# An eight-layer kernel whose expert routing moves into the layers beside it, in two halves, with three wide products split by columns

## The chip, the cores and the metric

One core of a Trainium2 chip runs the whole program. The metric is the device time of one execution in microseconds, taken as the median of several runs. The engines are TensorE (PE; its weight loads are shown as PEld), VectorE (DVE), ScalarE (ACT), GpSimd (POOL) and SyncE (SP, which starts DMAs). Each runs its own instructions in order and waits for the others on semaphores.

## The reference, cut to what matters

Sixteen sequences of 256 tokens with 128 channels go through eight residual layers: a wide attention (16 heads of 64), the experts, a "slope" attention, the same experts again, a "rope" attention, a "group" attention, a recurrence, and the group attention once more. The change touches the first four.

```python
x = x + _L0_attn_a_ref(_layernorm(x, axis=-1), ...)   # wide attention
x = x + _L0_ffn_ref(_layernorm(x, axis=-1), ...)      # experts
x = x + _L0_attn_b_ref(_layernorm(x, axis=-1), ...)   # slope attention
x = x + _L0_ffn_ref(_layernorm(x, axis=-1), ...)      # experts
x = x + _L1_attn_a_ref(_layernorm(x, axis=-1), ...)   # rope attention
...
def _L0_ffn_ref(x, gate_w, w1, w2):
    cap = int(EXPERT_CAPACITY * T / E)                # 64 of 256 tokens for each of 8 experts
    scores = jnp.einsum('BTC,CE->BTE', x, gate_w)
    probs = jax.nn.softmax(scores, axis=-1)
    probs_et = jnp.transpose(probs, (0, 2, 1))
    top_p, top_idx = jax.lax.top_k(probs_et, cap)
    xin = jnp.take_along_axis(x[:, None, :, :], top_idx[..., None], axis=2)
    h = jax.nn.gelu(jnp.einsum('BElC,ECH->BElH', xin, w1), approximate=False)
    y = jnp.einsum('BElH,EHC->BElC', h, w2)
    y = y * top_p[..., None]
    ...
```

Routing is everything down to `top_k`: each expert takes the 64 tokens of a sequence that like it most. A sequence ("batch" below) is routed without the others, but only after the layer in front has finished it.

## The kernel before

The activations `K.X` stay in on-chip memory for the whole program, as 32 tiles of 128 tokens by 128 channels, two tiles to a batch. Layers follow one another as blocks. A block begins when every engine has left the one before.

**Wide attention** (`wide_attention`, order from `wide_slots` and `wide_walk`). The heads are worked in 8 pairs for each of 16 batches; a pair is a slot. In a slot PE runs `score` (L2078, L2082), the row maxima of a later pair (`max`, L2062), `value` (L2093), the softmax sums (`sum`, L2099), and last the products of the coming batch that share two PSUM banks: `qk` (L2049, in every slot), `v` (L2055, four slots of eight), the transposes `norm` (L2043, slot 4), and the output product `project` (L2107, slots 3 and 5). In slot 7 the products stand ahead of `value`. All of it but `max`, `turnmax` and the shift `pick` is float32, and a float32 product is two PE instructions. `score` and `max` contract over 64 rows of the array, two side by side. `value` and `sum` fill 64 columns, two side by side. `qk`, `v`, `norm` and `project` use all 128 by 128.

**Routing** (`route`, a block of its own ahead of each experts' block). VectorE finishes the layer norm's statistics, normalizes all 32 tiles (L1463). PE transposes them (L1416), multiplies by the gate padded to 32 columns (L1423) and turns the logits back (L1431). VectorE does the softmax; PE turns the probabilities so that each of 128 partitions is one batch and expert. Then VectorE takes the 64 greatest in eight rounds of MAX8 and MATCH_REPLACE8 (L1492, L1493), turns the marks into slot numbers (L1494 to L1497), and PE turns those back (L1450). The probabilities and slots are `K.prob` and `K.slot`. Meanwhile ACT and POOL prepare the first two units of the experts (L1554, L1561 to L1564).

**Experts** (`experts`, order from `expert_schedule`). A unit is two batches. Step n has nine slots: `up` and `down` of unit n for each of 8 experts (L1636, L1644), and for unit n+1 the one-hot choice on VectorE (L1704) weighed on POOL (L1752), the gather (L1620) and four transposes (`turn`, L1627), and for unit n-1 the scatter (L1654). Step -1 only prepares unit 0. ACT does the GELU between `up` and `down`. At its start POOL first makes a counter and the constants of the coming attention (`pool_setup`).

**Slope attention** (`narrow_attention`, order from `NARROW_ORDER`). Eight slots for each batch, in which PE does `score` (L725, L732), `max` (L704, L711) and every second slot `value` (L745, 32 columns, four side by side); VectorE reduces the maxima (L911) and ACT takes the exponentials (L839). PE may not write new maxima before VectorE has reduced the old ones.

## Time and profile before

| what | value |
|---|---|
| median of 3 runs | 2300.91 us (2298.48 to 2302.19) |
| the profiled execution | 2305.23 us, span 2303.5 us |
| PE busy | 2030.9 us, 88% of the span |
| VectorE, ACT, POOL busy | 1557.1, 1174.0, 825.8 us |
| wide attention | from the start to about 655 us |
| routing and experts, first | about 656 to 880 us |
| slope attention | about 880 to 1124 us |
| routing and experts, second | from 1125 us |

The profiled execution is 4.3 us above the median of the runs, and its span lacks 1.7 us of its own time. Sums below are made on the span; what they take off it is taken off the median too. A matmul's row shows when it began and when its last result is there; since matmuls are pipelined, the distance from one row's start to the next row's start is what it took of PE.

### The profile page before, as it was taken

The page shows a single profiled execution, that of the slowest core. Times are in us where ns is not written, and L with a number is a line of the kernel's source. Part 1 is how long each engine was busy: PE and PEld are TensorE (multiplying, and loading weights), DVE is VectorE, ACT ScalarE, POOL GpSimd, SP SyncE. Part 2 cuts the span into 40 slices and gives each one's busy share as a digit, 9 for nine tenths or more (in the row PEclk, how much of TensorE's full clock was granted, in tenths as well). Part 3 has the DMA queues.
Part 4 walks back from the last instruction along what each step waited for, and adds up shares of the span by engine and source line. Part 5 has one row for each costly group of instructions (what it writes and reads, how often), then busy time and mean ns, then how long its engine had stood idle before and what let it go on. Part 6 is the DMA issues. An engine that isn't in the chain of part 4 may idle for free. (4 is left out here: it accounts for less than half of the span.)

```text
span 2303.5 us, 52488 instructions
## 1 busy us (share of the span) xinstructions
PE 2030.9 (88%) x20687; PEld 1356.6 (59%) x20687; DVE 1557.1 (68%) x2782; ACT 1174.0 (51%) x1972; POOL 825.8 (36%) x1276
## 2 busy tenths in 40 slices
PE   5999999999959997999589979997599985479996
PEld 3666666666638995665378966664345542335553
DVE  4777878787774444677554447775689965769983
ACT  3444444444323323666533326665478865447874
POOL 4444444444424341332144414440233322423330
PEclk9999999999979997999899989998699997769998
DMA  5000000000000011444000214440334420124441
GB/s 170 1 1 1 1 1 1 1 1 1 2 3 4 5 56 48 124 115 116 2 4 1 56 29 118 121 121 18 86 100 115 109 59 0 43 80 111 117 115 41
DMA packets 157126, 121.01 MB, mean 53 GB/s; under 512 B 13856, under 2 KB 129456, under 8 KB 156884
## 3 DMA queue, kind: packets, MB, share of 16 engines
q1 hardware_dynamic: 156884, 117.65, 18.9%
q8 instruction: 168, 2.75, 0.5%
q14 instruction: 74, 0.61, 0.1%
HBM read 63.48 MB, written 54.12 MB: 51 GB/s over the span
## 5 line engine op out<-in xcount | busy, mean ns | idle before, releaser
L911 DVE TENSOR_REDUCE l_group_mx<-maxima 128x4 f32<-128x1024 f32 x248 | 304.0, 1226 | 60.1 <-PE maxima L704 58.6
L839 ACT ACTIVATE l_group_pr<-scores 128x1024 f32<-128x1024 f32 x256 | 261.5, 1021 | 72.3 <-PE scores L725 69.9
L2195 POOL TENSOR_TENSOR l_wide_tiles_sum<-l_wide_pr 128x256 f32<-128x256 f32 x256 | 180.7, 727 | 212.4 <-ACT l_wide_pr L2138 212.4
L2166 DVE RECIPROCAL l_wide_rc<-bank 128x256 f32<-128x256 f32 x128 | 223.9, 1749 | 8.4 <-PE bank L2099 7.9
L2138 ACT ACTIVATE l_wide_pr<-scores 128x512 f32<-128x512 f32 x256 | 139.1, 595 | 163.1 <-PE scores L2082 163.1
L2150 DVE TENSOR_REDUCE l_wide_mx<-maxima 128x2 f32<-128x512 f32 x248 | 159.4, 685 | 52.7 <-PE maxima L2062 52.3
L2128 ACT ACTIVATE l_wide_qk<-bank 128x512 f32<-128x512 f32 x128 | 76.4, 597 | 174.9 <-PE bank L2049 174.8
L911 DVE TENSOR_REDUCE l_slope_mx<-maxima 128x6 f32<-128x768 f32 x124 | 118.9, 959 | 66.3 <-PE maxima L711 64.7
L911 DVE TENSOR_REDUCE l_rope_mx<-maxima 128x6 f32<-128x768 f32 x124 | 118.8, 958 | 44.0 <-PE maxima L711 42.8
L745 PE MATMUL bank<-l_group_pr,va 128*32 128x256 f32 x2048 | 143.9, 400 | 0.0
L839 ACT ACTIVATE l_slope_pr<-scores 128x768 f32<-128x768 f32 x128 | 103.5, 809 | 78.2 <-PE scores L732 78.0
L2093 PE MATMUL bank<-l_wide_pr,l_wide_va 128*64 128x256 f32 x1024 | 138.8, 392 | 0.0
L839 ACT ACTIVATE l_rope_pr<-scores 128x768 f32<-128x768 f32 x128 | 103.7, 810 | 64.7 <-PE scores L732 64.5
L2082 PE MATMUL scores<-l_wide_qk 64*128 64x256 f32 x1024 | 131.4, 376 | 0.0
L2190 POOL CAST l_wide_qk<-l_wide_qk 128x512 bf16<-128x512 f32 x128 | 78.1, 610 | 145.9 <-ACT l_wide_qk L2128 145.9
L704 PE MATMUL maxima<-l_group_st 50*128 50x256 bf16 x992 | 101.8, 285 | 30.8 <-DMA l_group_st<-mask_dram 15.0
L725 PE MATMUL scores<-l_group_st 53*128 53x256 bf16 x1024 | 103.0, 280 | 16.3 <-ACT l_group_pr L839 11.7
L1006 POOL CAST l_group_cols<-l_group_mx 128x32 bf16<-128x32 f32 x32 | 6.7, 209 | 307.7 <-DVE l_group_mx L911 307.7
L2082 PEld LDWEIGHTS scores<-l_wide_qk 64*128 64x128 f32 x1024 | 98.6, 189 | 9.8
L2049 PE MATMUL bank<-l_wide_xnt,w_q 128*128 128x256 f32 x256 | 90.3, 435 | 2.5 <-ACT l_wide_qk L2128 1.4
L1684 ACT ACTIVATE l_rope_e_ht<-maxima 128x512 f32<-128x512 f32 x64 | 38.2, 597 | 106.4 <-PE maxima L1636 106.0
L1684 ACT ACTIVATE l_slope_e_ht<-maxima 128x512 f32<-128x512 f32 x64 | 38.2, 597 | 104.0 <-PE maxima L1636 103.7
(478 smaller groups left out, 4779.6 us busy)
## 6 DMA issues: line engine op xcount, KB each, us to landing
l_group_st<-stack_dram SPq DMA_DIRECT2D x128, 192.0 KB, 3.9
l_slope_st<-stack_dram SPq DMA_DIRECT2D x64, 192.0 KB, 3.7
l_rope_st<-stack_dram SPq DMA_DIRECT2D x64, 192.0 KB, 3.8
stack_dram<-l_group_parts SPq DMA_DIRECT2D x64, 192.0 KB, 2.3
stack_dram<-l_group_parts SPq DMA_DIRECT2D x64, 128.0 KB, 1.9
stack_dram<-l_slope_parts SPq DMA_DIRECT2D x32, 192.0 KB, 2.4
stack_dram<-l_rope_parts SPq DMA_DIRECT2D x32, 192.0 KB, 2.3
stack_dram<-l_slope_parts SPq DMA_DIRECT2D x32, 128.0 KB, 2.2
```

Source lines behind the costliest of these rows:

```text
L704: ins = pe.matmul(Mx[:, z, first:first + keys], st[at, b % KEEP, 0, i, t * P:(t + 1) * P], st[at, b % KEEP, 1, i, 0:keys], start=(t == 0 o ...
L725: ins = pe.matmul(Tp[:, z, t * S:t * S + S - first], st[at, b % KEEP, 1, i, t * P:(t + 1) * P], st[at, b % KEEP, 0, i, first:S], start=(t ...
L745: ins = pe.matmul(Ob[i // 2][32 * z:32 * z + 32, (i % 2) * S + first:(i % 2) * S + S], va[:, b % KEEP, t, h // G, :], pr[:, (h // 2) % AHE ...
L839: act.activation(pr[:, i % AHEAD, :, 0:keys], Tp[:, :, 0:keys], ACT.Exp).then_inc(s["exps"], 1)
L911: dve.tensor_reduce(mx[:, b % 2, :, :, i], max_bank(i, b)[:, :, 0:BLOCKS * keys].rearrange("p z (a k) -> p z a k", k=keys), AX.X, ALU.max, ...
L2049: ins = pe.matmul(bank[:, z * S:(z + 1) * S], w[:, i * P:(i + 1) * P], xnt[:, at, :], start=True, stop=True)
L2082: ins = pe.matmul(Tb[z][:, t * S:(t + 1) * S], qk[rows(z), at, i, 1, t * P:(t + 1) * P], qk[rows(z), at, i, 0, :], start=False, stop=(t == ...
L2093: ins = pe.matmul(Ob[i % 2][rows(z), 0:S], va[:, at, kt, 2 * i + z, :], pr[:, i % 2, z, kt * S:(kt + 1) * S], start=(kt == 0), stop=(kt == ...
L2138: act.activation(pr[:, i % 2, z, :], Tb[z][:], ACT.Exp).then_inc(s["exps"], 1)
L2150: dve.tensor_reduce(mx[:, at, :, 2 * i + z], max_banks(i, b)[z][:].rearrange("p (t k) -> p t k", k=S), AX.X, ALU.max, negate=True).then_in ...
L2166: own.done(dve.reciprocal(rc[:], Ob[i % 2][:, S:2 * S]))
L2195: pool.tensor_tensor(tiles_sum[:, i % 2, z, :], pr[:, i % 2, z, 0:S], pr[:, i % 2, z, S:2 * S], ALU.add).then_inc(s["added"], 1)
```

## The change

The two routing blocks go. A new class `Route` does the same work for half of the batches, cut into pieces: `rstat` (statistics), `rnorm` (one batch's two tiles), `rturn` (transposes of two batches), `rgate` (logits of four), `rback` (turned back), `rsoft`, `rby`, `rtop.0` to `rtop.15` (the eight rounds, each two pieces), `rplace.0` to `.3` and `rslot`. Tables place every piece in a step and slot of another block. Batches 0 to 7 are routed inside the attention in front (`ROUTE_IN_WIDE`, `ROUTE_IN_SLOPE`, where the steps are the attention's batches), batches 8 to 15 inside the experts' block (`ROUTE_IN_EXPERTS`, where the steps are the experts' units). Statistics and normalizing are POOL's in the attentions and VectorE's among the experts, where POOL does only the power for the root. The reciprocal root is a power on POOL instead of ACT's root. PE's pieces share the two PSUM banks of the products. The rounds work on 64 partitions instead of 128, so both halves together have twice as many instructions of the same width. ACT and POOL now prepare units 0 and 1 at the experts' block's start, POOL after its setup and the power.

In the wide attention `qk`, `v` and `project` are each written as two products of 64 columns, into the upper and lower 64 partitions of the same bank.

```diff
--- before.py
+++ after.py
+ROUTED = NB // 2
+ROUTE_BANKED = ("rturn", "rgate", "rback", "rby", "rslot")
+ROUTE_ON = {"rturn": ("pe", "act"), "rgate": ("pe", "act"), "rback": ("pe", "dve"), "rsoft": ("dve", "act"),
+            "rby": ("pe", "dve"), "rtop": ("dve",), "rplace": ("dve",), "rslot": ("pe", "dve"), "rstat": ("norm",), "rnorm": ("norm",)}
...
+class Route:
...
+    def norm(self, eng, what, i, own):
+        K, s = self.K, self.s
+        if what == "rstat":
+            first = NT * (ROUTED * self.half + 4 * i)
+            tiles = slice(first, first + self.stat_tiles)
+            mean, spread, var, rstd, shift = (a[:, tiles] for a in (K.mean, K.spread, K.var, K.rstd, K.shift))
+            me, ve, mo, vo = (K.moments[:, tiles, n] for n in (1, 2, 4, 5))
+            self.settled(eng, ROUTED * self.half + 4 * i + 4)
+            if i == 0:
...
+            own.done(eng.tensor_tensor(mean, me, mo, ALU.add))
...
+            own.done(eng.tensor_tensor(var, var, spread, ALU.add))
+            if self.normed_on == "pool":
+                own.done(eng.tensor_tensor(rstd, var, self.power[:], ALU.pow))
+            else:
+                eng.sem_inc(s["var"], 1)
+                eng.wait_ge(s["root"], 1)
+            own.done(eng.tensor_tensor(shift, mean, rstd, ALU.mult))
+            eng.tensor_scalar(shift, shift, -1.0, None, ALU.mult).then_inc(s["norm"], 1)
+        else:
+            eng.wait_ge(s["norm"], 4 * NT * (i // 4) // self.stat_tiles + 1)
+            if i >= 2:
+                self.landed(eng, "rturn", i // 2 - 1)
+            for t in range(NT):
+                tile = NT * (ROUTED * self.half + i) + t
+                ins = eng.tensor_scalar(self.xn[:, i % 2, t, :], K.X[:, tile, :], K.rstd[:, tile:tile + 1],
+                                        K.shift[:, tile:tile + 1], ALU.mult, ALU.add)
+            ins.then_inc(s["xn"], 1)
...
+    def pe(self, pe, what, i, bank):
+        K, s = self.K, self.s
+        m, count = self.filling[what, i]
+        if what == "rturn":
+            pe.wait_ge(s["xn"], 2 * i + 2)
+            for t in range(2 * NT):
+                ins = pe.transpose(bank[:, t * P:(t + 1) * P], self.xn[:, t // NT, t % NT, :], K.ident[:])
+            ins.then_inc(self.full[m], 1)
...
+        elif what == "rgate":
+            pe.wait_ge(s["padded"], 1)
+            for n in range(2):
+                self.copied(pe, "rturn", 2 * i + n)
+            for j in range(4):
+                ins = pe.matmul(bank[32 * j:32 * j + 32, 0:S], self.gate[:], self.xnt[:, j // 2, (j % 2) * S:(j % 2 + 1) * S],
+                                start=True, stop=True)
+            ins.then_inc(self.full[m], 1)
...
+        elif what == "rtop":
+            if i == 0:
+                self.copied(dve, "rby", 0)
+            r = i // 2
+            if i % 2 == 0:
+                own.done(dve.max(self.top[0:64], self.work[r % 2][0:64]))
+            else:
+                own.done(dve.match_replace(self.work[(r + 1) % 2][0:64], self.top[0:64], self.work[r % 2][0:64], -1.0))
...
+ROUTE_IN_WIDE = placed([
+    (5, 6, "rstat.0"),
+    (5, 7, "rnorm.0"),
+    (6, 0, "rnorm.1"),
+    (6, 1, "rturn.0"),
...
+    (11, 5, "rtop.0"),
+    (11, 6, "rtop.1"),
...
+    (14, 2, "rslot.0"),
+])
+ROUTE_IN_SLOPE = placed([
+    (7, 6, "rstat.0"),
...
+    (13, 2, "rtop.0"),
...
+    (16, 1, "rslot.0"),
+])
+ROUTE_IN_EXPERTS = placed([
+    (-1, 0, "rstat.0"),
+    (-1, 1, "rnorm.0 rnorm.1 rturn.0 rnorm.2 rnorm.3 rturn.1 rgate.0"),
+    (0, 0, "rback.0"),
+    (0, 2, "rnorm.4 rnorm.5"),
+    (0, 3, "rturn.2 rnorm.6 rnorm.7"),
+    (0, 8, "rturn.3"),
+    (1, 0, "rgate.1"),
+    (1, 1, "rback.1 rsoft.0"),
+    (1, 3, "rsoft.1"),
+    (1, 8, "rby.0"),
+    (2, 0, "rtop.0"),
+    (2, 0, "rtop.1"),
...
+    (2, 7, "rtop.14"),
+    (2, 7, "rtop.15"),
+    (2, 8, "rplace.0 rplace.1 rplace.2 rplace.3 rslot.0"),
+])
...
-def route(nc, K, name, W, normed_unit, in_three):
...
+        if n < 0:
+            pieces += ROUTE_IN_EXPERTS.get((n, slot), [])
         if do_a:
             pieces += a.get(slot, [])
+        if n >= 0:
+            pieces += ROUTE_IN_EXPERTS.get((n, slot), [])
...
-        route(nc, K, name, W, normed, in_three)
...
+        routed = Route(nc, K, name + "_r", W, 1, sb, "dve", lambda eng, n: None, full, drained, filling)
...
-                        wait(pe, s["in_three"], n)
+                        wait(pe, s["in_three"], n + 2)
...
+            routed.root(pool)
+            for unit in range(2):
+                pool.wait_ge(s["xn"], unit + 1)
+                in_three(pool, own, unit).then_inc(s["in_three"], 1)
+                pool.wait_ge(s["in_three"], unit + 1)
...
                     for z, w in enumerate((W["wq"], W["wk"])):
-                        ins = pe.matmul(bank[:, z * S:(z + 1) * S], w[:, i * P:(i + 1) * P], xnt[:, at, :],
-                                        start=True, stop=True)
+                        for half in range(2):
+                            ins = pe.matmul(bank[rows(half), z * S:(z + 1) * S], w[:, i * P + half * D64:i * P + (half + 1) * D64],
+                                            xnt[:, at, :], start=True, stop=True)
...
-                    pe.matmul(bank[:], xnt[:, at, (i // 2) * P:(i // 2 + 1) * P],
-                              W["wv"][:, (i % 2) * 512:(i % 2 + 1) * 512], start=True, stop=True).then_inc(full[m], 1)
+                    for half in range(2):
+                        first = (i // 2) * P + half * D64
+                        ins = pe.matmul(bank[rows(half), :], xnt[:, at, first:first + D64],
+                                        W["wv"][:, (i % 2) * 512:(i % 2 + 1) * 512], start=True, stop=True)
+                    ins.then_inc(full[m], 1)
...
-                        ins = pe.matmul(bank[:, 0:C], att_t[:, at, c, i * P:(i + 1) * P], W["wo"][:, c, :],
-                                        start=(c == 0), stop=(c == PAIRS - 1))
+                        for half in range(2):
+                            first = i * P + half * D64
+                            ins = pe.matmul(bank[rows(half), 0:C], att_t[:, at, c, first:first + D64], W["wo"][:, c, :],
+                                            start=(c == 0), stop=(c == PAIRS - 1))
```

PE in the wide attention, batch 6, slot 1: a row is a product and `x` its count. Before (L2093 `value`, L2099 `sum`, L2049 `qk`, L2055 `v`, L2078 the next `score`):

```order
L2093 MATMUL bank4<-l0_wide_pr,l0_wide_va 64x256 x4
L2099 MATMUL bank4<-l0_wide_tiles_sum,ones 64x256 x2
L2049 MATMUL bank7<-l0_wide_xnt,w_q 128x256
L2049 MATMUL bank7<-l0_wide_xnt,w_k 128x256
L2055 MATMUL bank6<-w_v,l0_wide_xnt 128x512
L2078 MATMUL scores<-l0_wide_shift,pick 128x512 x2
```

PE at the same place after the change (L2309 `value`, L2315 `sum`, L2262 `qk`, L2270 `v`, L342 the routing's transposes, L2294 `score`):

```order
L2309 MATMUL bank4<-l0_wide_pr,l0_wide_va 64x256 x4
L2315 MATMUL bank4<-l0_wide_tiles_sum,ones 64x256 x2
L2262 MATMUL bank7<-l0_wide_xnt,w_q 64x256 x2
L2262 MATMUL bank7<-l0_wide_xnt,w_k 64x256 x2
L2270 MATMUL bank6<-w_v,l0_wide_xnt 64x512 x2
L342 MATMUL bank7<-ident,l0_wide_r_xn 128x128 x4
L2294 MATMUL scores<-l0_wide_shift,pick 128x512 x2
```

Each product of 128 columns has become two of 64, and `rturn.0` stands behind `v`.

PE at the start of the first experts' block, after the change (L342 `rturn`, L349 `rgate`, L1804 the gather of unit 0, L1820 `up`, L355 `rback`):

```order
L342 MATMUL bank6<-ident,l1_slope_e_r_xn 128x128 x4
L342 MATMUL bank7<-ident,l1_slope_e_r_xn 128x128 x4
L349 MATMUL bank6<-l1_slope_e_r_xnt,l1_slope_e_r_gate 32x256 x4
L1804 MATMUL bank6<-l1_slope_e_g,l1_slope_e_xs 128x512 x6
L1804 MATMUL bank7<-l1_slope_e_g,l1_slope_e_xs 128x512 x6
L1820 MATMUL maxima<-l1_slope_e_xi,w1 128x128 x4
L355 MATMUL bank7<-ident,l1_slope_e_r_work0 128x128 x2
```

Before, the gather was PE's first work in this block; now two `rturn` and an `rgate` of the second half stand ahead of it.

VectorE at the end of step 2 of the same block, after the change (L1903 a copy of `turn`, L414 and L416 the last round, L418 to L424 `rplace`, L426 the copy of `rslot`, L1907 `kept`):

```order
L1903 COPY l1_slope_e_gpt<-bank7 128x512
L414 MAX l1_slope_e_r_top<-l1_slope_e_r_work1 64x8
L416 MATCH_REPLACE l1_slope_e_r_work0<-l1_slope_e_r_top,l1_slope_e_r_work1 64x256
L418 TENSOR_SCALAR l1_slope_e_r_work1<-l1_slope_e_r_work0 64x256
L420 SCALAR_TENSOR_TENSOR l1_slope_e_r_xn<-l1_slope_e_r_work1 64x256
L422 TENSOR_TENSOR l1_slope_e_r_xn<-l1_slope_e_r_xn,l1_slope_e_r_work1 64x256
L424 TENSOR_SCALAR l1_slope_e_r_xn<-l1_slope_e_r_xn 64x256
L426 COPY slot<-bank7 128x2x64
L1907 COPY l1_slope_e_ys<-scores 128x512
```

On PE the `rslot` transposes of this place stand between the `down` of expert 6 and the `down` of expert 7. Before, the `turn` copy was followed by `kept` at once.

## Rows read from the trace of the kernel before

**Rows 1.** Busy time of each engine in two stretches (wide, slope attention).

```profile
core 0: us, PE busy (x) PEld busy (x) DVE busy (x) ACT busy (x) POOL busy (x), PEclk, DMA share, GB/s
300.00:400.00 100.00, 99.33 (x730) 64.18 (x730) 77.35 (x109) 42.63 (x79) 43.23 (x65) 1.00 0.01 1
1000.00:1100.00 100.00, 92.91 (x1543) 60.13 (x1540) 71.19 (x123) 64.51 (x101) 28.45 (x52) 1.00 0.40 109
```

**Rows 2.** Timeline of PE in a wide slot: start us, duration us, line, tiles, count.

```profile
305.65 1.08 PE L2093 MATMUL bank<-l_wide_pr,l_wide_va 128*64 128x256 f32 x8
306.56 0.60 PE L2099 MATMUL bank<-l_wide_tiles_sum,ones 128*64 128x256 f32 x4
307.10 0.70 PE L2049 MATMUL bank<-l_wide_xnt,w_q 128*128 128x256 f32 x2
307.63 0.59 PE L2049 MATMUL bank<-l_wide_xnt,w_k 128*128 128x256 f32 x2
308.06 1.02 PE L2055 MATMUL bank<-w_v,l_wide_xnt 128*128 128x512 f32 x2
```

**Rows 3.** Groups by line in the wide attention, 100 to 600 us.

```profile
L2107 PE MATMUL bank<-w_o,l_wide_att_t 128*128 128x128 f32 x400 | 48.7, 275 | 0.0
...
L2093 PEld LDWEIGHTS bank<-l_wide_pr,l_wide_va 128*64 128x64 f32 x824 | 50.0, 136 | 38.2 <-issue 20.6 <-DVE l_wide_att_t L2167 2.7
L2107 PEld LDWEIGHTS bank<-w_o,l_wide_att_t 128*128 128x128 f32 x400 | 48.6, 192 | 1.3
```

**Rows 4.** Timeline of the slope attention, PE and VectorE, at 1030 us.

```profile
1030.38 0.86 PE L745 MATMUL bank<-l_slope_pr,va 128*32 128x256 f32 x16
1031.17 0.34 PE L725 MATMUL scores<-l_slope_st 59*128 59x256 bf16 x4
...
1030.49 0.96 DVE L911 TENSOR_REDUCE l_slope_mx<-maxima 128x6 f32<-128x768 f32 x1 [0.55 <-PE maxima L711]
```

**Rows 5.** Timeline: each routing block's first and last row, and the experts' start.

```profile
656.27 0.13 POOL L1403 MEMSET l_slope_e_r_gate<- 128x32 f32 x1 [8.48 <-POOLq L2318]
...
685.43 0.42 DVE L1499 COPY l_slope_e_slot<-bank 128x256 f32<-128x256 f32 x1 [0.78 <-PE bank L1450]
686.90 0.18 POOL L1739 IOTA l_slope_e_count_i<- 128x64 int32 x1 [5.69 <-POOLq L1353]
...
693.46 8.04 POOL L1752 TENSOR_TENSOR l_slope_e_gp<-l_slope_e_g,l_slope_e_prob 128x512 f32<-128x512 bf16 x8
...
694.86 2.02 PE L1636 MATMUL maxima<-l_slope_e_xi,w 128*128 128x128 f32 x16 [0.78 <-ACT l_slope_e_xi L1679]
...
1125.34 0.12 POOL L1403 MEMSET l_rope_e_r_gate<- 128x32 f32 x1 [22.22 <-POOLq L488]
...
1156.61 0.19 POOL L1739 IOTA l_rope_e_count_i<- 128x64 int32 x1 [5.70 <-POOLq L1353]
...
1163.64 2.02 PE L1636 MATMUL maxima<-l_rope_e_xi,w 128*128 128x128 f32 x16 [0.78 <-ACT l_rope_e_xi L1679]
```

**Rows 6.** Timeline: pieces of the second routing block.

```profile
1127.51 8.29 DVE L1463 TENSOR_SCALAR l_rope_e_r_xn<-x,rstd,shift 128x128 f32<-128x128 f32 x32
...
1132.80 1.82 PE L1416 MATMUL maxima<-ident,l_rope_e_r_xn 128*128 128x128 f32 x8
...
1144.68 0.43 DVE L1492 MAX8 l_rope_e_r_top<-l_rope_e_r_work 128x8 f32<-128x256 f32 x1
...
1145.66 0.43 DVE L1492 MAX8 l_rope_e_r_top<-l_rope_e_r_work 128x8 f32<-128x256 f32 x1
...
1152.55 0.29 DVE L1494 TENSOR_SCALAR l_rope_e_r_taken<-l_rope_e_r_work 128x256 f32<-128x256 f32 x1
...
1155.13 0.42 DVE L1499 COPY l_rope_e_slot<-bank 128x256 f32<-128x256 f32 x1 [0.78 <-PE bank L1450]
```

**Rows 7.** The one power on POOL before each narrow attention: duration min/median/max ns, start us.

```profile
L1059 POOL TENSOR_TENSOR l_slope_first_norm<-l_slope_first_norm x1: 1040/1040/1040, 784.2 to 784.2; 128x4 f32<-128x4 f32 x1
```

**Rows 8.** Timeline: one-hot choice of one unit, and the first gather.

```profile
740.19 4.18 DVE L1704 TENSOR_TENSOR l_slope_e_g<-l_slope_e_count,l_slope_e_slot 128x512 bf16<-128x512 f32 x4
...
1158.62 4.24 PE L1620 MATMUL bank<-l_rope_e_g,l_rope_e_xs 128*128 128x512 bf16 x12 [3.52 <-DVE l_rope_e_g L1704]
```

453 lines of the change are left out of this document (289 added, 164 removed).

## The prediction

> **What bounds the kernel now.** First the busy shares by stretch [rows 1]: in the wide attention PE is busy 99.33 of 100 us, VectorE 77, ACT and POOL 43. There only PE's own time counts, and VectorE has about a fifth of its time free for other work. In the slope attention PE is at 93, VectorE at 71, ACT at 65, and PE and VectorE wait for each other slot by slot. Second, the timeline where one block ends and the next begins [rows 5]: the first routing block reaches from 656.27 to the experts' first row at 686.90, 30.6 us, the second from 1125.34 to 1156.61, 31.3 us. Nothing of another layer runs in them. Third, the order inside a wide slot [rows 2], since the edit there changes shapes and not work.
>
> **Column halves, in the wide attention.** From `qk`'s second product to `v` lies 0.43 us for two instructions of 256 columns, 0.215 each. `sum` has four of them, two side by side, so 0.43 of work, but `qk` starts 0.54 after it; and `qk`'s first product takes 0.53 where the second takes 0.43 [rows 2]. So going from 64-column to 128-column work costs 0.11 (PE runs empty) and 0.10 (the first weight load is not hidden), 0.21 together. After the change `sum` and `qk` have the same shape and the 0.21 goes. The halves themselves cost nothing if they overlap as `value`'s do: eight instructions in 0.91 are 0.114 each, half of 0.215 [rows 2]. In slot 4 the transposes `norm` behind `v` stay 128 wide and take the 0.21 back, and in slot 7 `turnmax` ahead of `qk` does. So six slots of eight gain: 93 places with a `qk` behind a `sum` (96 less those at the end), 93 x 0.21 = 19.5 us. The Trainium skill (TensorEngine Tiling (Array Packing), Key Properties) says that a change of tiling mode drains the engine while a change of tile within a mode doesn't; the 0.11 in the rows agrees with it.
>
> `project` is the doubtful product: 400 instructions took 48.7 us, 0.122 each, and their weight loads fill as much [rows 3]. It is bound by loads, and has now two loads of 64 columns for one of 128. A load's row is 136 ns long at 64 columns and 192 at 128 [rows 3]: 56 ns for 64 columns, 112 for two, against 122 now. I take no change. The lower end is 10 ns x 16 x 32 projects = 5 us gained. The upper end is that a half load can't be had faster than in `value`, 0.114: 32 x 0.114 = 3.65 us for 1.95, 54 us for 32 projects. The Trainium skill (TensorE: Matmul & The Clock Gate, LDWEIGHTS) puts a load at its columns over 1.2 GHz, 53 ns for 64; by that the sum would be 8 us lower, and no run here shows it yet.
>
> **Pieces of the first half in the wide attention.** On PE: 16 transposes at 0.122 = 2.0; eight `rgate` products of two instructions at 0.05 (16 four side by side take 0.79 [rows 4]) = 0.8; `rback`, `rby` and `rslot` eight transposes = 1.0; and 0.21 for seven changes of shape = 1.5. Together 5.3. Waits for the two shared banks, which ACT and VectorE empty: between 0 and 4, I take 2. VectorE gets eight rounds of 0.98 [rows 6], one half round a slot, beside its free fifth: nothing. POOL gets `rstat` and `rnorm`; a power of 4 elements took 1.04 us [rows 7], so one of 8 between 1.0 and 2.1, in a queue that is 57% free. What is queued behind it are POOL's sums of exponentials, needed about a slot later: nothing. Wide attention: -19.5 + 5.3 + 2 = -12 us.
>
> **First routing block.** It goes: -30.6. But the experts now start later. Before, the first `up` began 8.0 us after the block's first row [rows 5]. Now, counted from that row: VectorE does eleven small chained operations of at most 0.3 (one of 256 elements is 0.29 [rows 6]), 3.0 us. The power waits for POOL's setup, which before let the first weighing start at 6.6 [rows 5] while VectorE worked beside it; I take 4.5. The power of 16 elements lies between 1.0 and 4.2 (1.04, or 0.26 an element [rows 7]); I take the middle, 2.6: 7.1. Two small operations: 7.6. VectorE is held by it, and behind it stands the one-hot choice, 4.18 beside a busy POOL [rows 8], perhaps 2.5 alone; 3.4: 11.0. Four `rnorm` tiles at 0.26 (32 in 8.29 [rows 6]): 12.1. Then PE and VectorE take turns: `rturn` at the low clock 1.2 (eight transposes took 1.82 [rows 6]), `rnorm` 1.1, `rturn` 1.2, ACT's copy 0.8, `rgate` 1.1: 17.5. The gather that before stood first on PE: 4.24 [rows 8] to 5.3, 4.7, and ACT's copy 0.8: 23. So the first `up` comes 15 us later in its block; 9 and 20 are the ends, by the power and by the one-hot choice.
> Among the later slots PE is the bound (the `up` rows stand back to back), so its pieces add: `rback` twice, `rturn` twice, `rgate`, `rby`, `rslot`, 2.6 us. In step 2 PE's `rslot` waits for VectorE: behind the last `turn` come a copy (0.7), the last round (0.98), `rplace` to the slot copy 2.6 less its wait 0.8 [rows 6], and 0.2 for the signal, 3.7; PE has one `down` of 0.9 to cover it. 2.8 us of waiting. `up`, `down` of the last expert and with them `kept` stand behind. Sum: -30.6 + 15 + 2.6 + 2.8 = -10.2.
>
> **Second half of the same edit.** In the slope attention PE's pieces cost 3.8 as above and ten changes of shape 2.1: 5.9. VectorE idles 0.55 in a slot behind its reduction of 0.96 [rows 4], and a half round is 0.49: hidden in plain slots. In the slots that also hold `turn0`, `turn1`, `join` or two maxima it isn't; eight of sixteen, 0.4 each, 3 us, since PE may not write new maxima meanwhile. Waits for one bank and for `rback`: 1.5. Together +10, from 5 (PE alone) to 26 (all VectorE pieces, 12, PE's 5.9, and a slot's half for each of six hand-overs, 8). Second routing block: -31.3; start 14.5 later (POOL's setup is shorter there), 2.6 and 2.8 as before: -11.4.
>
> **Sum.** -12 - 10.2 + 10 - 11.4 = -24 us. Span 2303.5 to 2279.5; the median of the runs 2300.9 to 2277. Own range, by the ends of the start and of the slope attention: 2262 to 2290.
>
> **Rivals.**
> *The starts are cheap.* If the power takes its lower end and the gather runs warm, the first `up` is 9 us late instead of 15, twice, and the bank waits vanish: 2277 - 12 - 4 = 2261. For it: the chain is mine, link by link, and such links overlap. Against it: VectorE's order is strict, and the one-hot choice stands behind the power.
> *The slope attention pays in full.* VectorE becomes its bound and the upper end, 26 for 10, holds: 2293. For it: the 0.55 idle is scattered and is itself the time that PE's maxima take. Against it: 29% of VectorE is free there [rows 1].
> *Slower than before: half loads are no faster.* If each load of 64 columns takes 0.114 on PE, `project` costs 54 us more and the kernel goes to 2331. It decides from 0.086 us a load on: 24 us / 32 projects = 0.75, over 32 loads 0.024 more than 0.061 now. Loads at 0.072 would give 2277 + 11 = 2288. Against it: the 56 ns between the two loads' lengths [rows 3], and 16 loads and products of 32 columns in 0.79 [rows 4].
> *It doesn't do what it says:* the halves don't share the array, and the 19.5 isn't gained: 2297 without further loss. Against it is `value` [rows 2], same shape, same float32.
>
> **How the numbers follow.** Forecast 0.54; cheap starts 0.20; slope attention in full 0.12; half loads at or above 0.072 0.09, of which 0.04 above the point where it turns slower; halves without gain 0.05. A measurement of this kernel tells about 0.2%, 4.6 us, from no change. Faster by more: the forecast, the cheap starts, the slope case and the mild loads, 0.91. Within 0.2%: the halves without gain, 0.04. Slower: 0.05. The range reaches from 2254, past the cheap starts by the lower end of `project`, to 2293; what is left out is the two slower cases and some of each tail.
>
> **What would show it.** `sum` to `qk` at 0.43 and `qk`'s two halves at 0.43 each, project at 1.95 or below, a wide attention about 12 us shorter. No block between it and the experts; the first `up` 23 and 21.5 us after the block's first row; a PE gap of near 3 us ahead of `rslot` in step 2 of each experts' block. A slope attention 10 us longer, with its gaps on VectorE's reductions. I am wrong if the first `up` comes before 17, if `project` passes 2.7 us, or if the slope attention grows by over 20.

## The result

The changed kernel takes 2292.24 us, the median of seven runs (2287.71 to 2295.49); the kernel before took 2301.32 in seven runs (2298.25 to 2302.73). The ratio is 0.9966 with a 95% interval of 0.9955 to 0.9976: faster, by 9 us where 24 were forecast. The profiled execution has a span of 2290.5 us (2303.5 before). The stretches below add up to the difference of these spans, 13.0 us. The seven timed runs of a kernel lie within 4.5 us (before) and 7.8 us (after), and the profiled execution of the kernel before, 2305.23 us, is slower than all seven of its timed runs: the table takes the gain some us too high.

**Where the time went.** The span is cut at four instants that every variant has: VectorE's last `bn_stats` of the wide attention, PE's gather for the last unit in each of the two experts' blocks, and the first row of the second block (the routing block before, the experts' block after). 

| stretch, us (profiled executions) | before | after | difference | forecast |
|---|---|---|---|---|
| start to the wide attention's end | 654.6 | 642.5 | -12.1 | -12 |
| first block, to its last gather | 187.4 | 182.1 | -5.2 | -10.2 |
| slope attention, to the second block | 283.4 | 289.7 | +6.4 | +10 |
| second block, to its last gather | 187.7 | 188.3 | +0.6 | -11.4 |
| the rest | 990.5 | 987.9 | -2.6 | 0 |

The code of the last stretch is the same in all variants, and in the fourteen profiled executions of this study it lasted 983.3 to 990.5 us, with the kernel before at the top: its -2.6 lies inside that scatter.

**The wide attention** went as forecast. Busy time of 100 us of it, as in [rows 1]:

```profile
300.00:400.00 100.00, 98.97 (x946) 62.61 (x946) 77.80 (x110) 44.82 (x84) 44.46 (x66) 1.00 0.01 2
```

And a slot of the changed kernel on PE's timeline, as in [rows 2] (start us, duration us, line, tiles, count):

```profile
320.21 0.60 PE L2315 MATMUL bank<-l_wide_tiles_sum,ones 128*64 128x256 f32 x4
320.64 0.60 PE L2262 MATMUL bank<-l_wide_xnt,w_q 128*64 128x256 f32 x4
321.07 0.60 PE L2262 MATMUL bank<-l_wide_xnt,w_k 128*64 128x256 f32 x4
321.50 1.92 PE L2325 MATMUL bank<-w_o,l_wide_att_t 128*64 128x128 f32 x32
323.35 0.39 PE L2294 MATMUL scores<-l_wide_shift,pick 64*128 64x512 bf16 x2
```

From the products of `sum` to `w_q` now lie 0.43 us instead of 0.54, from `w_q` to `w_k` 0.43 instead of 0.53. `project`, the doubtful one, takes 1.85 us from its start to the next product (before, 1.95), 0.058 for a load of 64 columns and its product.

**The start of the experts** did not. The first block's first row is now at 644.04. What answers to [rows 5], on PE's timeline:

```profile
661.14 1.12 PE L342 MATMUL bank<-ident,l_slope_e_r_xn 128*128 128x128 f32 x4 [19.40 <-DVE l_slope_e_r_xn L327]
...
668.12 3.88 PE L1804 MATMUL bank<-l_slope_e_g,l_slope_e_xs 128*128 128x512 bf16 x12 [0.50 <-ACT l_slope_e_r_work L381]
672.78 1.13 PE L1820 MATMUL maxima<-l_slope_e_xi,w 128*128 128x128 f32 x8 [0.78 <-ACT l_slope_e_xi L1867]
```

On VectorE's (L1898 is the one-hot choice, L327 `rnorm`):

```profile
651.05 0.56 DVE L319 TENSOR_TENSOR shift<-mean,rstd 128x16 f32<-128x16 f32 x1 [4.42 <-POOL rstd L334]
...
651.73 5.24 DVE L1898 TENSOR_TENSOR l_slope_e_g<-l_slope_e_count,slot 128x512 bf16<-128x512 f32 x4
656.88 4.20 DVE L327 TENSOR_SCALAR l_slope_e_r_xn<-x,rstd,shift 128x128 f32<-128x128 f32 x4
662.37 2.22 DVE L327 TENSOR_SCALAR l_slope_e_r_xn<-x,rstd,shift 128x128 f32<-128x128 f32 x4 [1.29 <-PE bank L342]
664.52 2.48 DVE L1898 TENSOR_TENSOR l_slope_e_g<-l_slope_e_count,slot 128x512 bf16<-128x512 f32 x4
```

On POOL's (L334 the root, L1736 to L1739 the splitting in three, of which eight rows stand from 650.97 to 659.9, L1946 the weighing):

```profile
648.08 2.93 POOL L334 TENSOR_TENSOR rstd<-var,l_slope_e_r_power 128x16 f32<-128x16 f32 x1
...
653.92 1.48 POOL L1739 TENSOR_TENSOR l_slope_e_xs<-l_slope_e_rest,l_slope_e_xs 128x512 bf16<-128x512 f32 x1
...
656.50 1.48 POOL L1737 TENSOR_TENSOR l_slope_e_rest<-l_slope_e_xn,l_slope_e_xs 128x512 f32<-128x512 f32 x1
658.04 0.61 POOL L1738 CAST l_slope_e_xs<-l_slope_e_rest 128x512 bf16<-128x512 f32 x1
658.73 1.15 POOL L1739 TENSOR_TENSOR l_slope_e_xs<-l_slope_e_rest,l_slope_e_xs 128x512 bf16<-128x512 f32 x1
659.96 4.04 POOL L1946 TENSOR_TENSOR l_slope_e_gp<-l_slope_e_g,prob 128x512 f32<-128x512 bf16 x4
```

The first `up` (672.78) comes 28.7 us after the first row, against 8.0 before: 20.8 later, where 15 were forecast. In the second block it is 28.6 against 7.0, 21.6 later for 14.5. The root is in time (VectorE's shift begins 7.0 after the first row; the forecast had 7.1). Behind it the four one-hot instructions take 5.24 us beside POOL's splitting of the first two units and 2.48 without it (664.52). The first four `rnorm` tiles take 4.20 us, 1.05 each, where [rows 6] has 0.26 each with POOL idle, and the next four 2.22. Meanwhile PE waits 19.40 us.

**Step 2 of the experts.** PE's timeline at the places, `rslot`, of both blocks:

```profile
743.56 0.31 PE L365 MATMUL bank<-ident,l_slope_e_r_xn 64*128 64x64 f32 x2 [2.70 <-DVE l_slope_e_r_xn L424]
...
1216.90 0.45 PE L365 MATMUL bank<-ident,l_rope_e_r_xn 64*128 64x64 f32 x2 [4.54 <-DVE l_rope_e_r_xn L424]
...
1219.15 3.19 PE L1820 MATMUL maxima<-l_rope_e_xi,w 128*128 128x128 f32 x14
```

VectorE's ahead of the second one:

```profile
1210.49 0.48 DVE L1210 TENSOR_SCALAR l_rope_w<-bank 128x64 f32<-128x64 f32 x2
1211.01 0.87 DVE L1216 COPY l_rope_w<-bank 128x32 f32<-128x32 f32 x4
...
1216.47 0.28 DVE L424 TENSOR_SCALAR l_rope_e_r_xn<-l_rope_e_r_xn 64x256 f32<-64x256 f32 x1
```

Busy time behind it (columns as in [rows 1]; the granted clock is third from the right):

```profile
1210.00:1215.00 5.00, 2.37 (x22) 2.18 (x20) 4.49 (x20) 1.08 (x2) 1.16 (x1) 1.00 0.00 0
1215.00:1220.00 5.00, 3.10 (x14) 3.01 (x15) 2.48 (x6) 0.00 (x0) 0.00 (x0) 0.65 0.01 3
1220.00:1225.00 5.00, 5.00 (x47) 4.78 (x48) 4.25 (x5) 1.19 (x2) 4.17 (x3) 0.66 0.00 0
```

The wait of 2.70 us in the first block is the 2.8 of the forecast. In the second it is 4.54, since VectorE also prepares the rope attention's weights there (L1210, L1216: 3 us from 1210.49), between two rounds; and behind it the granted clock falls. The means of 0.65 and 0.66 hide its two levels (1.2 and 2.4 GHz): in windows of one or two us it is 1.00 until 1216, while PE already stands still, 0.50 from 1217 to 1223, and 1.00 again from 1224 on. Step 2 lasts 32.1 us from gather to gather in this block (24.3 before), 26.0 in the first (22.8 before).

### The profile page after: what moved, and what is told of

It is laid out like the page before. It is cut to its first block and busy times, and to the rows that moved or that the text cites. A ratio compares the mean times of both kernels' runs of the same rounds, so it can differ in the third digit from the quotient of the medians.

```text
span 2290.5 us, 54970 instructions
## 1 busy us (share of the span) xinstructions
PE 2007.0 (88%) x21847; PEld 1335.6 (58%) x21847; DVE 1575.7 (69%) x2826; ACT 1174.6 (51%) x1972; POOL 862.9 (38%) x1356
## 5 line engine op out<-in xcount | busy, mean ns | idle before, releaser
L2309 PE MATMUL bank<-l_wide_pr,l_wide_va 128*64 128x256 f32 x1024 | 138.0, 390 | 0.0
L1025 PE MATMUL maxima<-l_group_st 50*128 50x256 bf16 x992 | 102.0, 285 | 28.6 <-DVE l_group_mx L1238 15.1
L2309 PEld LDWEIGHTS bank<-l_wide_pr,l_wide_va 128*64 128x64 f32 x1024 | 63.3, 136 | 45.6 <-issue 22.3
```

The costliest lines, as they stand in the source:

```text
L1025: ins = pe.matmul(Mx[:, z, first:first + keys], st[at, b % KEEP, 0, i, t * P:(t + 1) * P], st[at, b % KEEP, 1, i, 0:keys], start=(t == 0 o ...
L2309: ins = pe.matmul(Ob[i % 2][rows(z), 0:S], va[:, at, kt, 2 * i + z, :], pr[:, i % 2, z, kt * S:(kt + 1) * S], start=(kt == 0), stop=(kt == ...
```

## Theory and rivals

*Theory.* The column halves gain what was forecast; what is missing was lost in the experts' blocks, at two places. (1) At the start VectorE and POOL hold each other up: one-hot and `rnorm` on one side, the splitting in three on the other, and the first gather stands behind both. (2) In step 2 the last places are ready too late, behind VectorE's other work.
*Rivals.* (a) The chain of root, `rnorm`, turn and gate ahead of the gather is by itself longer than forecast, and POOL is no part of it. (b) The loss lies in the attention layers, where VectorE's rounds push the maxima. (c) The halves gain less than thought, and the routing costs less.

All variants below were timed beside the kernel before, on three chips; its median there was between 2299.6 and 2301.6 us, so the ratio compares better than the median. The stretches, cut as in the table above and in us, come from one profiled execution each. From the slope attention to the second block the code of the changed kernel is the same as that of ten variants (all but e_halves and e_slope_rounds), and that stretch still lies between 289.5 and 291.9:

| variant | median | ratio (95%) | wide | block 1 | slope | block 2 | rest |
|---|---|---|---|---|---|---|---|
| before | | 1 | 654.6 | 187.4 | 283.4 | 187.7 | 990.5 |
| after | 2292.2 | 0.9966 (0.9955-0.9976) | 642.5 | 182.1 | 289.7 | 188.3 | 987.9 |
| e_halves | 2279.1 | 0.9913 (0.9898-0.9928) | 636.6 | 187.3 | 281.5 | 188.3 | 983.3 |
| e_nohalves | 2307.8 | 1.0041 (1.0029-1.0053) | 661.1 | 186.2 | 291.3 | 186.7 | 984.8 |
| e_slope_rounds | 2286.4 | 0.9946 (0.9931-0.9962) | 643.3 | 182.7 | 289.1 | 186.8 | 987.3 |
| e_pool_late | 2282.2 | 0.9919 (0.9896-0.9942) | 643.0 | 178.7 | 289.8 | 182.7 | 987.0 |
| e_pool_split | 2285.6 | 0.9932 (0.9916-0.9949) | 642.6 | 181.4 | 291.9 | 182.5 | 987.1 |
| e_rounds | 2290.1 | 0.9955 (0.9939-0.9972) | 643.2 | 181.3 | 291.6 | 185.9 | 989.4 |
| e_rounds0 | 2282.2 | 0.9915 (0.9901-0.9929) | 642.4 | 179.5 | 291.7 | 181.1 | 986.0 |
| e_late | 2288.0 | 0.9949 (0.9934-0.9964) | 643.1 | 184.4 | 290.9 | 186.0 | 984.2 |
| e_both | 2285.6 | 0.9937 (0.9919-0.9954) | 643.0 | 181.6 | 290.1 | 185.7 | 984.1 |
| e_best | 2279.7 | 0.9913 (0.9898-0.9928) | 643.3 | 176.4 | 289.8 | 179.3 | 989.0 |
| e_best2 | 2265.4 | 0.9848 (0.9828-0.9868) | 643.6 | 172.9 | 290.5 | 173.9 | 983.3 |
| e_best3 | 2253.9 | 0.9807 (0.9791-0.9822) | 642.9 | 166.9 | 289.5 | 168.6 | 984.0 |

## Halves alone, and routing alone

e_halves is the kernel before with the three products cut in column halves; e_nohalves is the changed kernel with these edits taken back. The edit, at `qk` (it is alike at `v` and `project`; lines that the code breaks are joined):

```
-    ins = pe.matmul(bank[:, z * S:(z + 1) * S], w[:, i * P:(i + 1) * P], xnt[:, at, :], start=True, stop=True)
+    for half in range(2):
+        ins = pe.matmul(bank[rows(half), z * S:(z + 1) * S], w[:, i * P + half * D64:i * P + (half + 1) * D64],
+                        xnt[:, at, :], start=True, stop=True)
```

Expected of e_halves: 

> The kernel before with the column halves alone, all routing as it was. If the halves bring what the weight loads in the rows say, the wide attention is 19.5 us shorter and the whole 2281 to 2282 us; if VectorE's shift takes part of it back, since TensorE now arrives earlier, 2284 to 2288; if halves bring nothing by themselves, 2301.

Expected of e_nohalves: 

> The changed kernel with whole weight loads as before, all of the routing moved. If the routing pieces in the wide attention cost 7.4 us and the halves 19.5, the wide attention ends 19.5 us later than in the changed kernel and the whole takes 2311 to 2312 us; if the pieces cost more and hide behind the halves' gain, the difference is smaller, 2304 to 2308.

The last `bn_stats` of the wide attention, on VectorE's timeline, in e_halves:

```profile
636.35 0.29 DVE L2180 BATCH_NORM_STATS2 moments<-x 128x6 f32<-128x128 f32 x1
```

In e_nohalves:

```profile
660.79 0.29 DVE L2390 BATCH_NORM_STATS2 moments<-x 128x6 f32<-128x128 f32 x1
```

The halves shorten the wide attention by 18.0 us alone and by 18.6 with the routing pieces in it; the pieces cost 5.8 with halves and 6.5 without. So rival (c) falls: both terms are near the forecast (19.5, and 5.3 + 2), each a little smaller, so that the two errors cancel in the -12. The whole is the surprise. The halves alone are 20.5 us faster than before, the whole change 9; the routing alone is 8.2 us slower than before (2307.8 against 2299.6), with an interval of 1.0029 to 1.0053 that leaves 1 out. The change is a gain and a loss put together, and its routing half makes the kernel slower. The forecast's own terms had that half at 7.3 - 10.2 + 10 - 11.4 = -4.3.

## Is it the slope attention?

e_slope_rounds leaves out fourteen of the sixteen round halves of ROUTE_IN_SLOPE:

```
     (13, 2, "rtop.0"),
     (13, 3, "rtop.1"),
-    (13, 4, "rtop.2"),
...
-    (15, 1, "rtop.15"),
     (15, 2, "rplace.0"),
```

> The changed kernel, with fourteen of the sixteen round halves of the slope attention's routing left out (the slots that follow from it are then not the reference's). The slope attention lasted 283.4 us before and 289.7 after from the seventh gather of the experts in front to the next block's start. If VectorE's rounds carry 3 of the 6.3 us, as the forecast had it, the stretch is 286.7 and the whole 2289 us; if TensorE's pieces carry all of it and VectorE has the room, the stretch stays at 289 to 290 and the whole at 2292; if VectorE's rounds carry all of it, 284 and 2286.

The slope attention lasts 289.1 us, 0.7 less than in the changed kernel; variants with the same slope code differ by more than that (289.5 to 291.9). So VectorE has room for most of the rounds, and a cost of a us or two is not excluded. The median, 2286.4, would by itself fit the case in which the rounds carry everything (2286). It is not this stretch that shows it: the profiled execution is the slowest of the four (2290.8), and what made the others faster was not profiled. Busy time of the whole stretch (columns as in [rows 1]), in e_halves, then in the changed kernel, then in e_slope_rounds:

```profile
823.98:1105.52 281.54, 250.52 (x3754) 171.24 (x3751) 166.78 (x301) 157.29 (x250) 66.41 (x122) 0.95 0.31 85
```

```profile
824.61:1114.35 289.74, 254.84 (x3794) 174.09 (x3791) 176.47 (x338) 160.31 (x256) 81.54 (x162) 0.95 0.31 83
```

```profile
825.97:1115.02 289.05, 255.03 (x3794) 174.28 (x3791) 171.06 (x317) 160.21 (x256) 81.19 (x163) 0.95 0.31 83
```

Without the rounds VectorE's 176.5 us of work fall to 171.1 and the other engines' stay. PE has 254.8 us of work instead of 250.5, 4.3 more, and idles 34.9 us instead of 31.0. So the pieces on PE carry 4 us of what the stretch costs, 6.4 us against the kernel before and 8.2 against e_halves, and waits around them the rest. By line, PE's waits grow most ahead of `rturn` (1.2 us, for POOL's normalising), ahead of the transposes of `l_slope_cols`, which POOL makes (1.0), and of `l_slope_ot` (0.7), and by 0.5 ahead of the maxima (e_halves against the changed kernel). Rival (b) does not explain what is missing: the stretch costs about what was forecast (10) or less.

## The start: VectorE against POOL

e_pool_late takes the overlap away and leaves everything else; e_pool_split does so for the second unit only:

```
             routed.root(pool)
+            pool.wait_ge(routed.s["xn"], 4)        # e_pool_late
             for unit in range(2):
                 pool.wait_ge(s["xn"], unit + 1)
+                if unit == 1:                      # e_pool_split, without the line above
+                    pool.wait_ge(routed.s["xn"], 4)
                 in_three(pool, own, unit).then_inc(s["in_three"], 1)
```

Expected of e_pool_late: 

> The changed kernel, except that POOL starts its in_three operations of the first two units only once VectorE has written all four normalised batches of the first group (rnorm.0 to rnorm.3), so that onehot and the eight rnorm instructions run with nothing beside them on POOL. Theory A (VectorE is slowed by POOL's work beside it): onehot falls from 5.24 us for four to about 2.5, each rnorm instruction from 1.05 us to 0.26 to 0.55, the last rnorm ends some 6 to 8 us earlier than 664.6; the first `up` then comes 22 to 27 us after the block's start instead of 28.7, since the gather still has to wait for in_three, and the whole takes 2280 to 2290 us. Theory B (the chain of root, rnorm, turns and gate ahead of the gather is long by itself, POOL is no part of it): the rnorm instructions stay at 1.05 us and the gather comes behind in_three by 4 us more, first `up` 31 to 33 us after the start, 2297 to 2302 us.

Expected of e_pool_split: 

> The changed kernel, except that POOL starts in_three of unit 1 (not of unit 0) only once VectorE has written rnorm.3. In e_pool_late the gather began 3.08 us after TensorE was free for it, since POOL's in_three of unit 0 came last. If contention between the two engines is the cause of the late start, the four onehot instructions stay slow beside unit 0's in_three (about 5 us), the rnorm instructions are short (1.1 us for four), and the first gather starts 20 to 21 us after the block's start (24.1 in the changed kernel, about 19.3 in e_pool_late): 2283 to 2287 us. If it were the wait alone, without contention, that helped, the gather would start no earlier than in the changed kernel: 2291 to 2293.

e_pool_late on VectorE's timeline (the block's first row is at 644.53):

```profile
651.84 2.49 DVE L1898 TENSOR_TENSOR l_slope_e_g<-l_slope_e_count,slot 128x512 bf16<-128x512 f32 x4
654.25 1.10 DVE L327 TENSOR_SCALAR l_slope_e_r_xn<-x,rstd,shift 128x128 f32<-128x128 f32 x4
656.64 1.12 DVE L327 TENSOR_SCALAR l_slope_e_r_xn<-x,rstd,shift 128x128 f32<-128x128 f32 x4 [1.29 <-PE bank L342]
```

On PE's:

```profile
655.40 1.12 PE L342 MATMUL bank<-ident,l_slope_e_r_xn 128*128 128x128 f32 x4 [13.17 <-DVE l_slope_e_r_xn L327]
...
663.87 4.62 PE L1804 MATMUL bank<-l_slope_e_g,l_slope_e_xs 128*128 128x512 bf16 x12 [3.08 <-issue]
```

On POOL's:

```profile
657.82 2.81 POOL L1736 CAST l_slope_e_xs<-l_slope_e_xn 128x512 bf16<-128x512 f32 x1 [6.31 <-DVE l_slope_e_r_xn L327]
```

e_pool_split on VectorE's (first row at 644.19):

```profile
651.86 4.82 DVE L1898 TENSOR_TENSOR l_slope_e_g<-l_slope_e_count,slot 128x512 bf16<-128x512 f32 x4
656.61 1.10 DVE L327 TENSOR_SCALAR l_slope_e_r_xn<-x,rstd,shift 128x128 f32<-128x128 f32 x4
```

And on PE's:

```profile
663.64 4.86 PE L1804 MATMUL bank<-l_slope_e_g,l_slope_e_xs 128*128 128x512 bf16 x12 [0.50 <-ACT l_slope_e_r_work L381]
```

With POOL still, the four one-hot instructions take 2.49 us (5.24) and four `rnorm` 1.10 (4.20). PE's first turn comes at 655.40 instead of 661.14, 5.7 us earlier in the program. The gather then waits 3.08 us for POOL (the row names no releaser, but `in_three` of unit 0 ends there), whose first cast takes 2.81 us beside VectorE's next one-hot (0.61 in the changed kernel without it): the same thing the other way round. In e_pool_split the one-hot instructions are slow again beside unit 0 (4.82) and the `rnorm` quick (1.10), and the gather starts at 663.64, 19.5 us after the block's first row (24.1 in the changed kernel). Rival (a) falls: its rows would have stayed at 1.05 us. An added wait has made the kernel faster, by 10 and 7 us (0.9919 and 0.9932 against 0.9966). That e_pool_split's first block is nevertheless only 0.7 us shorter in the table comes from a low clock in its step 2 (next section).

The Trainium skill (SBUF — State Buffer, Who interferes with whom) has the rule: VectorE and GpSimd share a pair of ports under an exclusive lock. A VectorE instruction with two SBUF inputs contends with a GpSimd instruction that reads SBUF; a copy or a `tensor_scalar` contends in a 2-port mode, and then whoever issues first has the pair for its whole instruction. One-hot is of the first kind, and `rnorm` can be of the second.

The rows of the changed kernel agree. Read in windows of one us, the four `rnorm` from 656.88 on end at 658.05, 658.72, 659.96 and 661.08. POOL's instructions beside them end at 657.98, 658.65, 659.88 and, the first of the weighing, 661.00. Each `rnorm` ends 0.07 or 0.08 us behind one of POOL's: 1.05 us is not a slower `rnorm` but one that is through only when POOL's instruction is.

## Step 2: the places come last

e_rounds moves the rounds to the front of step 2 and the places to slot 6; e_rounds0 has the places in slot 5 and gives `rslot` the other bank. Both edits in short, in one fence:

```
+    (2, 0, "rtop.0 rtop.1"), (2, 1, "rtop.2 rtop.3 rtop.4"), (2, 2, "rtop.5 rtop.6 rtop.7"),
+    (2, 3, "rtop.8 rtop.9 rtop.10 rtop.11 rtop.12 rtop.13"),
+    (2, 4, "rtop.14"), (2, 5, "rtop.15"), (2, 6, "rplace.0 rplace.1 rplace.2 rplace.3"),   # e_rounds
+    (2, 4, "rtop.14 rtop.15"), (2, 5, "rplace.0 rplace.1 rplace.2 rplace.3"),              # e_rounds0
+    (2, 8, "rslot.0"),
+    EXPERT_BANK: "rslot": (0,)                                                             # e_rounds0
```

Expected of e_rounds: 

> The changed kernel with the sixteen round halves of the experts' blocks moved to the front of step 2 (2, 3, 3, 6, 1 and 1 in slots 0 to 5, the four places in slot 6, the turn back rslot in slot 8 as before). If TensorE's waits of 2.70 and 4.54 us on VectorE's place, and the fall of the granted clock behind the second, come from the place being reached last, both waits go and the clock stays at 1.00 there: 2292 - 2.7 - 4.5 - 3 = about 2282 us. Rival: the rounds delay VectorE's copies of the turns in slots 4 to 7 instead, and TensorE waits there as long: 2290 to 2293.

Expected of e_rounds0: 

> The changed kernel with only the experts' step 2 altered: rounds in slots 0 to 4 (2, 3, 3, 6 and 2), the places in slot 5 and rslot in slot 8 on bank 0 instead of bank 1. In e_rounds (places in slot 6, bank 1) TensorE still waited in front of rslot, 1.6 us in the first block and 3.70 us in the second, for VectorE's copy of the last turn, which fills the same bank and stood behind the places and the setup of the attention behind. If that is all that was left, step 2 falls from 25.95 and 32.13 us to 23.4 and 24.6 and the whole to 2292 - 10 = about 2282 us. If the second block's step stays above 28 us, VectorE's setup work itself, not the order and the bank, sets it: 2288 to 2290.

PE's timeline at the end of step 2 of the second block in e_rounds:

```profile
1217.64 0.34 PE L365 MATMUL bank<-ident,l_rope_e_r_xn 64*128 64x64 f32 x2 [3.70 <-DVE l_rope_e_gpt L1894]
```

And in e_rounds0 (`rslot` and the `down` behind it, with no wait):

```profile
1212.04 0.33 PE L365 MATMUL bank<-ident,l_rope_e_r_xn 64*128 64x64 f32 x2
1212.30 1.16 PE L1818 MATMUL scores<-w,l_rope_e_ht 128*128 128x128 f32 x8
```

e_rounds missed its forecast (2290 for 2282, near the rival that it named): only 1.1 and 2.2 us of step 2 went. The wait stayed, 3.70 us, but its releaser is another: VectorE's copy of the last turn (L1894). `rslot` fills the same bank as that turn, and the copy now stands behind the places and the rope weights. With the other bank and the places one slot earlier, no wait is left in e_rounds0, step 2 falls from 26.0 to 23.2 and from 32.1 to 24.6 us, and the whole to 2282.2, where 2282 were expected. Theory (2) is shown, with its share: about 10 us of the whole, of which the forecast had counted 2 x 2.8. In the second block the 7.6 us are the wait (4.5) and the work behind it at the low clock (3.0, by subtraction).

The low clock is in part luck. Six executions have the same wait of 2.70 us ahead of `rslot` in the first block. Their step 2 lasts 25.95 us in the changed kernel, 25.96 in e_pool_late and e_slope_rounds, 27.55 in e_late, and 28.89 and 28.93 in e_pool_split and e_nohalves. In e_pool_split the clock is 1.00 at 738 to 739 and 0.50 from 740 to 746, behind this row:

```profile
740.06 0.45 PE L365 MATMUL bank<-ident,l_slope_e_r_xn 64*128 64x64 f32 x2 [2.70 <-DVE l_slope_e_r_xn L424]
```

So the same wait costs between nothing and 3 us on top of itself. In the second block, with 4.54 us of waiting, step 2 lasts 30.6 to 32.1 in these executions: always some of it, and never the same.

## Routing behind the first gather

e_late takes the routing out of the way of the first gather; e_both adds e_rounds:

```
-    (-1, 0, "rstat.0"),
-    (-1, 1, "rnorm.0 rnorm.1 rturn.0 rnorm.2 rnorm.3 rturn.1 rgate.0"),
+    (-1, 3, "rstat.0"),
+    (0, 2, "rnorm.0 rnorm.1"), (0, 3, "rturn.0 rnorm.2 rnorm.3 rturn.1"), (0, 8, "rgate.0"),
+    (1, 0, "rback.0 rnorm.4 rnorm.5"), (1, 1, "rturn.2 rnorm.6 rnorm.7"), (1, 3, "rturn.3"),
+    (1, 5, "rgate.1"), (1, 6, "rback.1 rsoft.0"), (1, 7, "rsoft.1"), (1, 8, "rby.0"),
...
-            routed.root(pool)
             for unit in range(2): ... in_three ...
+            routed.root(pool)
```

Expected of e_late: 

> The changed kernel with no routing piece ahead of the first gather: rstat stands behind the first gather, rnorm.0 to rnorm.3, rturn.0, rturn.1 and rgate.0 in step 0, the second group in step 1, and POOL takes the root behind the two in_three. The rounds stand as before in step 2. If the late start of the experts is what the pieces ahead of the gather cost, the first `up` comes 11 to 14 us after the block's start instead of 28.7, and steps 0 and 1 grow by the 2 to 4 us of TensorE's pieces that were outside them: 2292 - 2 x 13 = about 2266 us (2260 to 2272). Rival: steps 0 and 1 become too full, TensorE waits there for ScalarE's and VectorE's copies, and half of it is given back: 2275 to 2282.

Expected of e_both: 

> The pieces of e_late and the rounds of e_rounds together. If the two causes are separate and sum, 2266 - 10 = about 2256 us (2250 to 2264). If one hides the other or step 1 is too full, 2265 to 2275.

e_late in the first block, on PE's timeline:

```profile
659.18 2.02 PE L1813 MATMUL maxima<-l_slope_e_xi,w 128*128 128x128 f32 x16 [0.78 <-ACT l_slope_e_xi L1860]
665.70 1.94 PE L1804 MATMUL bank<-ident,l_slope_e_gp 128*128 128x128 f32 x8 [4.50 <-POOL l_slope_e_gp L1939]
...
672.42 2.76 PE L1797 MATMUL bank<-l_slope_e_g,l_slope_e_xs 128*128 128x512 bf16 x12 [0.35 <-DVE l_slope_e_gpt L1896]
```

And on POOL's:

```profile
657.64 2.93 POOL L334 TENSOR_TENSOR rstd<-var,l_slope_e_r_power 128x16 f32<-128x16 f32 x1
660.54 9.91 POOL L1939 TENSOR_TENSOR l_slope_e_gp<-l_slope_e_g,prob 128x512 f32<-128x512 bf16 x8
```

Both missed, by over 20 us. The first `up` does come early (659.18, 14.6 us after the first row, 14 earlier than in the changed kernel). But POOL now splits two units in three and takes the root before it weighs the first unit, and PE waits 4.50 us for that; the second gather is only 6.5 us earlier than in the changed kernel, and steps 0 and 1 lose it again. They are 7.7 us longer; PE's waits in them are two of 1.4 and 1.7 us for a `rnorm` just issued and three of 0.8, two of those where a routing piece takes the bank that a turn has just filled. I had counted the wait that goes, and not the one behind it.

## A version that beats both

e_best orders POOL's start by need, and keeps the banks apart; e_best2 and e_best3 each move what the profile of the one before showed as PE's longest wait. In short, with `in_three` the splitting and `gp` the weighing of a unit:

```
# POOL: in_three(0); [root in e_best]; gp(0); in_three(1); [root in e_best2]; gp(1); [root in e_best3]; setup of the attention behind
# e_best:  (-1, 3) rstat.0, (0, 0) rnorm.0 rnorm.1 rturn.0, (0, 1) rnorm.2 rnorm.3, (0, 3) rturn.1, (0, 8) rgate.0
# e_best2: (-1, 3) rstat.0, (0, 2) rnorm.0 rnorm.1, (0, 3) rturn.0 rnorm.2 rnorm.3, (0, 8) rturn.1 rnorm.4 rnorm.5, (1, 0) rgate.0
# e_best3: (0, 2) rstat.0 rnorm.0 rnorm.1, (0, 4) rturn.0, (0, 5) rnorm.2 rnorm.3, (0, 8) rturn.1 rnorm.4 rnorm.5, (1, 0) rgate.0
# all: second group and softmax in step 1, nearly as in e_late, banks chosen anew; rounds and rslot as in e_rounds0
```

Expected of e_best: 

> The changed kernel with the experts' start rebuilt: onehot and the gather come first, POOL makes in_three of unit 0, the root, gp of unit 0 and only then in_three of unit 1, its work for the attention behind waits until gp of unit 1 is issued; the first group's pieces are spread over steps 0 and 1 (rnorm from slot 0 of step 0), the turned batches and the gate use the bank that the slot's turn does not, the rounds stand in slots 0 to 4 of step 2, the places in slot 5 and rslot uses bank 0. If e_late lost its early start to POOL's order (TensorE waited 4.50 us for gp behind two in_three and the root) and to pieces that take the bank just filled (five waits of 0.8 to 2.7 us), all of this is gone: first gather 6 to 8 us after the block's start instead of 24.1, second gather 20 to 23 us after the start instead of 34.9, steps 1 and 2 at 23 to 24.5 us instead of 24.7 and 26, and the whole 2292 - 2 x (12 + 3) = about 2262 us (2255 to 2270). Rival: POOL and VectorE slow each other wherever their work falls together, so that the order only moves the loss: 2275 to 2285.

Expected of e_best2: 

> The kernel of e_best with two further moves: POOL takes the root behind in_three of unit 1 instead of ahead of gp of unit 0, and the first group's pieces stand later (rturn.0 in slot 3 of step 0, rturn.1 in slot 8, rgate.0, rback.0 and rturn.2 in slots 0 and 1 of step 1). In e_best TensorE waited 8.04 us for the first normalised batch and 1.69 us for the third in front of rturn; if those waits are what is left of the late start, the second gather comes 20 to 22 us after the wide attention's end instead of 29.8, step 1 is 1 to 2 us shorter, and the whole is 2280 - 2 x 9 = about 2262 us (2258 to 2268), below both the kernel before with column halves alone (2279) and e_best. Rival: POOL's chain of in_three, gp, in_three, gp is what the second gather waits for, so that only 2 to 4 us a block come: 2272 to 2276.

Expected of e_best3: 

> The kernel of e_best2 with the statistics of the routing taken out of the start: rstat.0 and the first two rnorm stand in slot 2 of step 0, rturn.0 in slot 4 on bank 1, rnorm.2 and rnorm.3 in slot 5, and POOL takes the root behind gp of unit 1. In e_best2 TensorE waited 5.68 us in step 0 for VectorE's copy of the turned gp, which stood behind onehot of unit 1 and that behind the wait for the root. If this wait is the root's, it goes, the second gather comes 19 to 21 us after the wide attention's end instead of 25.7, and the whole is 2265 - 2 x 5 = about 2255 us. Rival: VectorE and TensorE then wait for the root in slots 2 to 4 instead, and nothing is won: 2263 to 2267.

The longest wait on PE's timeline in the first block's start, in e_best:

```profile
665.99 1.09 PE L342 MATMUL bank<-ident,l_slope_e_r_xn 128*128 128x128 f32 x4 [8.04 <-DVE l_slope_e_r_xn L327]
```

In e_best2:

```profile
667.44 1.97 PE L1802 MATMUL bank<-ident,l_slope_e_gp 128*128 128x128 f32 x8 [5.68 <-DVE l_slope_e_gpt L1894]
```

In e_best3, with the second gather:

```profile
662.48 2.76 PE L1795 MATMUL bank<-l_slope_e_g,l_slope_e_xs 128*128 128x512 bf16 x12 [0.35 <-DVE l_slope_e_gpt L1894]
...
670.72 0.63 PE L342 MATMUL bank<-ident,l_slope_e_r_xn 128*128 128x128 f32 x4 [1.47 <-DVE l_slope_e_r_xn L327]
```

e_best missed (2279.7 for 2262) and fell on its rival, by which the order only moves the loss; but PE waited 8.04 us there for the first normalised batch, and the next two runs, which change only the order and the banks, rule that rival out. Moving the pieces behind gave 14 us (2265.4), and taking the statistics and the root out of VectorE's queue ahead of the second one-hot gave 11.5 more: 2253.9, 0.9807 of the kernel before, against 0.9913 for the halves alone. In e_best3 the first block is 20.5 us shorter than before and the second 19.1; the second gather comes 19.6 us after the wide attention's end (36.4 in the changed kernel). The same routing work, in the same layers, is then worth some 25 us over the halves alone, where in the changed kernel it costs 13.

## Why the prediction was wrong

**Right.** The wide attention: -12.1 for -12, both its terms right to 1.5 us and the rest of the agreement luck, since their errors cancel. The removed blocks, the root at 7.0 us for 7.1, the wait of 2.7 for 2.8 in the first block's step 2, and PE's pieces (from the first `up` on, the first block grew by 4.8 us to the slope attention's first maxima, for 5.4). That nothing came on top of that wait was luck too, by the other executions with the same wait.

**The start, mis-sized.** The step "VectorE is held by it, and behind it stands the one-hot choice ... 3.4 ... Four `rnorm` tiles at 0.26" failed. One-hot took 5.24, the two sets of four `rnorm` 4.20 and 2.22 where 1.05 and 1.1 stood: 6.1 us, the whole of the 5.8 by which the first `up` was later than forecast (and 7.1 in the second block). The 0.26 came from a row [rows 6] in which POOL had nothing to do, and the changed kernel puts exactly these instructions beside POOL's heaviest stretch. For the one-hot choice the forecast had 4.18 beside a busy POOL [rows 8] and took the middle between that and its own guess of 2.5 alone, though POOL was sure to be busy; 2.5 is right for POOL still (2.49), and beside the splitting even 4.18 was too low. The second block has the same three durations. e_pool_late shows the cause and gives 10 us back.

**Step 2 of the second block, mis-sized.** The forecast took it over from the first block: 2.6 and 2.8 "as before". It grew by 10.4 us from the first `up` on, for 5.4, since VectorE also prepares the rope attention there, and the longer gap brought the clock down. e_rounds0, in which wait and fall are both gone, shows it.

**The slope attention** cost 6.4 for 10: the rounds, counted at 3, cost 0.7 in the one pair of executions that shows it, and PE's pieces 4 for 5.9. The same code took up to 2.2 us more in other variants, so part of these 3.6 is scatter.

The sum by this: -24, and +5.8 and +7.1 at the starts, +5.0 in the second step 2, -3.6 in the slope attention, -2.6 in the rest, -0.7 for small differences: -13.0, the difference of the spans.

**The range and the rivals.** The forecast's own range, "by the ends of the start and of the slope attention", ends at 2290. Its terms reach further: 5 and 5 us more at the starts and 16 in the slope attention are 26 on top of 2277, which is 2303. The terms thus allowed that nothing is gained. The time fell on the one in which the slope attention pays in full (2293), but for another reason: that stretch was cheap. The case that mattered was not among them: that the routing half as a whole costs more than it removes. The forecast had it at -4.3 us, and the expected loss of the starts alone (15 and 14.5 us of each 31 removed) was reason to price the two halves of the change apart.

## What to carry to other kernels

How long a VectorE instruction of these kinds takes depends on what the engine on the other side of the lock does at that time: where a change puts VectorE's and POOL's work side by side, take durations from a stretch where both run. Where there is none, an estimate from these rows is to count each short VectorE instruction as long as one of POOL's beside it (`rnorm` 1.05 us and one-hot 1.31, beside POOL instructions of 0.61 to 1.48). Here, moving a block's work into the head of the next one paid only once it stood behind the first instructions that the bottleneck engine needs: order every engine's queue there by who is waited for, look at the profile, and move the next wait. And measure the parts of a change apart: here a gain of 20 us hid a loss of 8 to 13.

## What the runs showed of the hardware

- VectorE's smallest operations suffer most. On its timeline in e_best2, operations on 16 elements take 0.17 us, and 0.96 while POOL weighs (four instructions in 4.04 us from 651.53 on); one passes for each of POOL's, as with `rnorm` above:

```profile
649.56 0.17 DVE L306 TENSOR_TENSOR mean<-moments 128x16 f32<-128x16 f32 x1
...
651.63 0.97 DVE L310 TENSOR_TENSOR spread<-spread 128x16 f32<-128x16 f32 x1
652.64 0.96 DVE L311 TENSOR_SCALAR spread<-spread 128x16 f32<-128x16 f32 x1
```

- The power on POOL took 2.93 us for 16 elements a partition, where that of 4 elements took 1.04 [rows 7].
- Halving the columns of three products, so that they have the shape of their neighbours, gave 18 us in the wide attention and cost nothing in weight loads (0.058 us for a load of 64 columns with its product).
- In the changed kernel a gap of 4.54 us on PE was followed by over six us at a granted clock of 0.50. Gaps of 2.70 us were followed by no fall in three executions, by about six us at 0.50 in two (e_pool_split, e_nohalves) and by a shorter fall in one (e_late). The price of such a gap is not fixed: steps of the same code with the same gap differed by up to 3 us.
